# Expert results added in memory by the indirect stores, into three sums per token

## The chip, the cores and the metric

One core of a Trainium2 chip runs the whole program. The metric is the device time of one execution in microseconds (us); lower is better. The time of a kernel is the median of its runs.

## The reference, cut to what matters

One decoder layer over 16 sequences of 128 tokens with 256 features: a self-attention block, a cross-attention block and a feed-forward block, each followed by a layer norm. The change touches the last one, a mixture of 32 experts of which every token uses four, plus a shared expert:

```python
topk_idx, topk_w = _route(tokens, router_weight, router_bias)     # 4 of 32 experts per token
gate_vals = jax.nn.silu(jnp.einsum('th,eih->tei', tokens, gate_w))
up_vals = jnp.einsum('th,eih->tei', tokens, up_w)
expert_out = jnp.einsum('tei,ehi->teh', gate_vals * up_vals, down_w)
sel = jnp.take_along_axis(expert_out, topk_idx[:, :, None], axis=1)
mixed = (sel * topk_w[:, :, None]).sum(1)                          # the sum over the token's 4 experts
x = _layernorm(x + mixed + shared)
```

All 2048 tokens are routed; 2048 x 4 = 8192 expert results of 256 fp32 values (1 KB) have to be summed by token.

## The kernel before, in words

The kernel doesn't compute every expert for every token. During cross-attention each token's row is stored four times into the DRAM table `x_rows`, sorted by expert, by indirect stores that GpSimd issues (`scatter`, L1394). A row has 258 words: 256 words of token, then the row number where its result has to go, then its routing weight. Rows of an expert that no token fills are copies of a padding row, built in `padrow` (L343 to L345) and written to `pad_block` and to the end of `x_rows` by SyncE at the end of the first stage (L338, L339).

The expert stage (`expert_layer`) then runs over NT = 95 tiles of 128 rows: tile n < 32 is the first tile of expert n ("by expert"); the other 63 are taken from a table that the kernel works out ("by table"), with unused ones at the end that hold padding alone. For each tile, in a software pipeline over all engines:

- SyncE loads the tile's 129 KB of rows from `x_rows` into `xg` (L2081, 15 buffers).
- TensorE transposes the rows (L2304), multiplies by the expert's gate and up weights (L2255 by expert, L2286 by table), transposes the hidden values (L2296), multiplies by the down weights (L2315).
- ScalarE copies and applies silu (L2122, L2131, L2136). VectorE multiplies, splits into high and low halves (L2205, L2217), copies each tile's destination row numbers into `ix` (L2201) and moves the result from PSUM to `yo` (L2195, L2197; 8 buffers, each reused once the store that read it has landed, by the semaphore `stored`).
- GpSimd issues one indirect store per tile (L2097): row p of `yo` goes to row `ix[p]` of the DRAM table `y_rows`. Every (token, expert) pair has a row of its own, 4 per token. Padding rows have destination 1 << 20, which is over the bounds check, so that nothing is stored for them.

GpSimd does nothing else in this stage, and its instructions run in order.

When all 95 stores have landed, SyncE starts the tail (L2084 to L2089): 16 loads of 512 KB, one per 128 tokens, each with the four results of each token side by side, into four buffers `yg`. For each of these tiles GpSimd adds results 0 and 1 (`ya`, L2105), VectorE adds results 2 and 3 (`yb`, L2227), and TensorE sums three terms in PSUM by multiplying with the identity: `xs` (the residual with the shared expert in it, L2323), `ya` (L2325), `yb` (L2327). VectorE takes mean and variance (L2233 to L2239), GpSimd the inverse root (`frstd`, L2110), VectorE the shift (L2244), ScalarE scales (L2144) and stores 128 KB of output (L2146).

Of the kernel before, what the change touches and what calls it, by code (L numbers as in the profile page):

```python
# [6 lines left out]
F32 = mybir.dt.float32  # L7
F16 = mybir.dt.float16
BF16 = mybir.dt.bfloat16
ALU = mybir.AluOpType  # L10
# [3 lines left out]
U32 = mybir.dt.uint32  # L14

P = 128
D = 256
KT = D // P
NB = 16
# [9 lines left out]
TOPK = 4  # L29
# [9 lines left out]
NT = NE + NB * TOPK - 1  # L39
CAP = NB * P + P  # L40
BLOCKS = CAP // P
NDEST = NB * P * TOPK
RW = D + 2
PAD_DEST = 1 << 20
PAD = -3e38
TAKEN = 3e38
QK_SCALE = float(HD) ** -0.5
# [36 lines left out]
def wait(eng, sem, value):  # L84

    if not isinstance(value, int) or value > 0:
        eng.wait_ge(sem, value)


def live(n, count=NB):  # L90
    return 0 <= n < count
# [29 lines left out]
def decoder_kernel(nc, x, ctx_t, wcat, vecs, rowvecs, rel_bias, consts, masks, experts, rbias_d, out):  # L121
# [3 lines left out]
    with es:  # L125
# [5 lines left out]
        def sem(name):  # L131

            stage_sems.append(nc.alloc_semaphore(name=name))
            return stage_sems[-1]
# [32 lines left out]

        x_rows = nc.dram_tensor("x_rows", ((NE * BLOCKS + 1) * P, RW), U32, kind="Internal").ap()
        pad_block = nc.dram_tensor("pad_block", (P, RW), U32, kind="Internal").ap()
        y_rows = nc.dram_tensor("y_rows", (NDEST, D), F32, kind="Internal").ap()  # L170
        x_tiles = x.rearrange("b p d -> p b d")
        w_tiles = wcat.rearrange("(k p) c -> p k c", p=P)

        padded = sem("padded")
        idb_r = sem("idb_r")
        rc_in, k_in, id16_r, front_set = sem("rc_in"), sem("k_in"), sem("id16_r"), sem("front_set")
        ctx_in = [sem(f"ctx_in{k}") for k in range(2)]
# [19 lines left out]
        with ExitStack() as st:  # L197
# [107 lines left out]
            with nc.Block() as block:  # L305
                @block.sync
                def _(sp):
                    def piece(c):
                        t, col, width = W_PIECES[c]
                        wait_split(sp, c - WB)  # L310
                        sp.dma_start(wst[:, c % WB, :, 0:width], w_tiles[:, :, t * W1COLS + col:t * W1COLS + col + width]).then_inc(w_in[c % WB], 16)

                    sp.dma_start(xs[:, 0], x_tiles[:, 0]).then_inc(x_first, 16)
                    sp.dma_start(ident[:], consts[:, 0:P]).then_inc(const_in, 16)
                    sp.dma_start(vec[:], vecs).then_inc(const_in, 16)
                    sp.dma_start(par[:], masks).then_inc(const_in, 16)
                    sp.dma_start(rows[:, 4 * D:5 * D], rowvecs[4 * D:5 * D].rearrange("(a n) -> a n", a=1).broadcast_to([P, D])).then_inc(const_in, 16)
                    sp.dma_start(xs[:, 1:4, :], x_tiles[:, 1:4, :]).then_inc(x_in[0], 16)
                    for c in range(3, NPROJ):
                        piece(c)  # L320
                    sp.dma_start(xs[:, 4:8, :], x_tiles[:, 4:8, :]).then_inc(x_in[1], 16)
                    sp.dma_start(rows[:, 0:4 * D], rowvecs[0:4 * D].rearrange("(a n) -> a n", a=1).broadcast_to([P, 4 * D])
                                 ).then_inc(rows_in, 16)
                    sp.dma_start(rel[:].rearrange("p g h k -> p (g h k)"), rel_bias).then_inc(rel_in, 16)
                    for c in range(NPROJ, len(W_PIECES)):
                        piece(c)
                        if c in (8, 10):
                            k = {8: 2, 10: 3}[c]
                            sp.dma_start(xs[:, 4 * k:4 * k + 4, :], x_tiles[:, 4 * k:4 * k + 4, :]).then_inc(x_in[k], 16)
                    for n in range(FRONT):  # L330
                        sp.dma_start(cst[:, n], ctx_tiles[:, :, n]).then_inc(ctx_in[n], 16)
                    sp.dma_start(tri[:], consts[:, P:2 * P]).then_inc(rc_in, 16)
                    sp.dma_start(known[:], consts[:, 2 * P + NE:2 * P + 2 * NE + 1]).then_inc(k_in, 16)
                    sp.dma_start(first[:], consts[:, 2 * P:2 * P + NE]).then_inc(rc_in, 16)
                    sp.dma_start(dest_f[:].rearrange("p n k -> p (n k)"), consts[:, 2 * P + 2 * NE + 1:]).then_inc(rc_in, 16)
                    sp.dma_start(rbias[:], rbias_d.rearrange("(a n) -> a n", a=1).broadcast_to([P, NE])).then_inc(rc_in, 16)
                    sp.wait_ge(pad_set, 3)
                    sp.dma_start(pad_block, padrow[:]).then_inc(padded, 16)  # L338
                    sp.dma_start(x_rows[NE * CAP:NE * CAP + P, :], padrow[:]).then_inc(padded, 16)  # L339

                @block.gpsimd
                def _(pool):
                    pool.memset(padrow[:, 0:D], 0).then_inc(pad_set, 1)  # L343
                    pool.memset(padrow[:, D:D + 1], PAD_DEST).then_inc(pad_set, 1)
                    pool.memset(padrow[:].bitcast(F32)[:, D + 1:D + 2], 0.0).then_inc(pad_set, 1)  # L345
                    pool.memset(neghalf[:], -0.5).then_inc(setup, 1)
                    pool.memset(share[:], 2.0 / P).then_inc(setup, 1)
# [794 lines left out]
        c = Shared()  # L1142
# [10 lines left out]
        c.xv, c.xv_heads = xv, xv_heads  # L1153
        c.we_hi, c.we_lo = ([sb(f"{name}{j}", [P, 2, NE * EI], F16) for j in range(KT + 1)] for name in ("we_hi", "we_lo"))
        c.count = sb("count", [P, NE])
        c.pad_block, c.padded = pad_block, padded
        c.scattered = [sem(f"scattered{k}") for k in range(RR)]
        c.fill_row, c.fill_r, c.filled = sb("fill_row", [P, NE], U32), sem("fill_r"), [sem(f"filled{k}") for k in range(PAD_GROUPS)]
        cross_attention(nc, c, ctx_t, experts, consts, rbias_d, out)
# [806 lines left out]
def expert_layer(nc, c, st, consts, out):  # L1966
# [9 lines left out]
    L_GT, L_GU, L_SILU, L_TR = 2, 3, 4, 5  # L1976
    L_HI, L_DN, L_YO = (5, 6), (7, 8), (8, 9)
    LAG3 = L_YO[1]
    YS = 4

    def s3(name, shape, dt=F32):
        return st.enter_context(nc.sbuf_tensor(name, shape, dt))
# [29 lines left out]

    words = c.xT[:].rearrange("p n s k t -> p (n s k t)").bitcast(U32)
    xg = words[:, 0:G * RW].rearrange("p (g w) -> p g w", g=G)
    yg = words.bitcast(F32).rearrange("p (q d) -> p q d", q=YS)
    ya = s3("ya", [P, 2, D])
    yb = s3("yb", [P, 2, D])
    fin = s3("fin", [P, 4, D])
    fstats = s3("fstats", [P, 2, 6])
    fmv = s3("fmv", [P, 4, 2])  # L2020
# [7 lines left out]
    gu_ps, eg_r, eh_r, ehhi_r, ehlo_r = sem("gu_ps"), sem("eg_r"), sem("eh_r"), sem("ehhi_r"), sem("ehlo_r")  # L2028
    dn_ps, yo_r = sem("dn_ps"), sem("yo_r")
    stored = [sem(f"stored{k}") for k in range(YO)]  # L2030
    y_in = [sem(f"y_in{k}") for k in range(YS)]
    ya_r, yb_r, ysum_ps, fshift_r = sem("ya_r"), sem("yb_r"), sem("ysum_ps"), sem("fshift_r")
    f_stat, f_mv, f_var, f_rstd, fin_r = sem("f_stat"), sem("f_mv"), sem("f_var"), sem("f_rstd"), sem("fin_r")
    sent = [sem(f"sent{k}") for k in range(4)]

# [7 lines left out]
    def xg_word(dt, q, w):  # L2043
        return xg[:, q, D + w:D + w + 1].bitcast(dt)

    ix_r = sem("ix_r")
    tr_ps = sem("tr_ps")

    def by_expert(n):
        return live(n, NE)  # L2050
# [7 lines left out]
    def on_sync(sp, read_up_to, pad_rows):  # L2058
# [24 lines left out]
        for q in range(YO):  # L2083
            sp.wait_ge(stored[q], 16 * len(range(q, NT, YO)))  # L2084
        for n in range(NB):
            wait(sp, ya_r, n - YS + 1)
            wait(sp, yb_r, n - YS + 1)
            sp.dma_start(yg[:, n % YS], c.y_rows[n * P * TOPK:(n + 1) * P * TOPK, :].rearrange("(p k) d -> p (k d)", k=TOPK)
                         ).then_inc(y_in[n % YS], 16)  # L2089
        for p in range(4):  # L2090
            sp.wait_ge(sent[p], 16 * NB // 4)

    def on_gpsimd(pool):
        for n in range(NT):
            pool.wait_ge(ix_r, n + 1)
            pool.wait_ge(yo_r, n + 1)
            pool.indirect_dma_start(c.y_rows, bass.IndirectOffsetOnAxis(ap=ix[:, n % IX], axis=0),  # L2097
                                    yo[:, n % YO], None, bounds_check=NDEST - 1, oob_is_err=False).then_inc(stored[n % YO], 16)

        def final(i, p, h):  # L2100
            n = i
            if live(n):
                pool.wait_ge(y_in[n % YS], 16 * (n // YS + 1))
                wait(pool, ysum_ps, n - 1)
                pool.tensor_tensor(ya[:, n % 2], yg[:, n % YS, 0:D], yg[:, n % YS, D:2 * D], ALU.add).then_inc(ya_r, 1)  # L2105
            n = i - 2
            if live(n):
                pool.wait_ge(f_var, n + 1)
                wait(pool, fin_r, n - 3)
                pool.tensor_tensor(frstd[:, n % 4], fvar[:, n % 2], neghalf[:], ALU.pow).then_inc(f_rstd, 1)  # L2110

        unrolled(2, final)
# [72 lines left out]
    def on_vector(dve):  # L2185
        def tile(i, s, h):
# [11 lines left out]
            n = i - L_IX  # L2198
            if live(n, NT):
                dve.wait_ge(gathered[n % G], 16 * (n // G + 1))  # L2200
                dve.tensor_copy(ix[:, n % IX], xg_word(U32, n % G, 0)).then_inc(ix_r, 1)  # L2201
            for n in due(i, L_HI):
                dve.wait_ge(ehhi_r, n + 1)
                wait(dve, dn_ps, n - U + 1)
# [15 lines left out]
        unrolled(LAG3, tile, NT)  # L2220

        def final(i, p, h):
            n = i
            if live(n):
                dve.wait_ge(y_in[n % YS], 16 * (n // YS + 1))
                wait(dve, ysum_ps, n - 1)
                dve.tensor_tensor(yb[:, n % 2], yg[:, n % YS, 2 * D:3 * D], yg[:, n % YS, 3 * D:4 * D], ALU.add).then_inc(yb_r, 1)  # L2227
            n = i - 1
            if live(n):
                q = n % 2  # L2230
# [17 lines left out]
    def on_tensor(pe, shared_done):  # L2248
# [72 lines left out]
        for n in range(NB):  # L2321
            wait(pe, fin_r, n - 3)
            pe.matmul(SUM_BANK[n % 4][:, 0:D], ident[:], xs[:, n], start=True, stop=False)  # L2323
            pe.wait_ge(ya_r, n + 1)
            pe.matmul(SUM_BANK[n % 4][:, 0:D], ident[:], ya[:, n % 2], start=False, stop=False)  # L2325
            pe.wait_ge(yb_r, n + 1)
            pe.matmul(SUM_BANK[n % 4][:, 0:D], ident[:], yb[:, n % 2], start=False, stop=True).then_inc(ysum_ps, 1)  # L2327

    layer = Shared()
    layer.on_sync, layer.on_gpsimd, layer.on_scalar, layer.on_vector, layer.on_tensor = on_sync, on_gpsimd, on_scalar, on_vector, on_tensor  # L2330
# [18 lines left out]
def host_arrays(a):  # L2349
# [18 lines left out]
    place = np.arange(P, dtype=np.float32)  # L2368
    eye, earlier = np.eye(P, dtype=np.float32), (place[:, None] < place[None]).astype(np.float32)
    first_row = np.arange(NE, dtype=np.float32) * CAP  # L2370
    dest = ((np.arange(NB)[None, :, None] * P + np.arange(P)[:, None, None]) * TOPK + np.arange(TOPK)).reshape(P, NB * TOPK)
    consts = np.concatenate([eye, earlier, np.tile(first_row + 1, (P, 1)), place[:, None],
                             np.tile(np.arange(NE, dtype=np.float32), (P, 1)), dest], axis=1).astype(np.float32)

# [7 lines left out]
```

## Time and profile before

| | |
|---|---|
| time, median of 3 runs | 708.2 us (704.61 to 708.8) |
| the profiled execution: span from its first to its last instruction | 703.0 us; no other time of it is given |
| TensorE busy in the span | 579.9 us (82%) |
| VectorE, ScalarE, GpSimd busy | 515.3, 482.2, 475.9 us |
| indirect stores of results, L2097 | 95, 93.9 us busy, 988 ns each |
| first and last of them start at | 532.44 and 658.88 us |
| first tail load issued | 661.14 us |

The last instructions' stores to the output end after the last instruction that the span counts; what lies around the span is the difference between it and a run's time. The mean granted TensorE clock over the span is 0.948 of full speed.

### The profile page before, as it was taken

Reading aid. Unit: us, or ns where it says so; the run is one execution under the profiler, and the core shown is the slowest. Engines: PE = TensorE matmul, PEld = TensorE weight load, DVE = VectorE, ACT = ScalarE, POOL = GpSimd, SP = SyncE. Lnnn points to the kernel's source line nnn. Section 1 sums busy time; section 2 is a strip of 40 time slices with the busy share of each in tenths; the row PEclk is TensorE's granted clock in tenths of the full one; section 3 lists DMA queues with packets and bytes.
Section 4 is the critical chain, followed back from the end, with each engine's and each line's share of the span. In section 5 each row is a group of like instructions: output and inputs, shape, how many; then the busy total and the mean of one; then the engine's idle time right before and its main releaser. Section 6 shows DMA issues by size and latency. Waiting matters only on the chain.

```text
span 703.0 us, 24581 instructions
## 1 busy us (share of the span) xinstructions
PE 579.9 (82%) x8258; PEld 481.6 (69%) x8258; DVE 515.3 (73%) x2067; ACT 482.2 (69%) x1325; POOL 475.9 (68%) x622
## 2 busy tenths in 40 slices
PE   1799999999999864888888888766668999999393
PEld 1578888888888653656566656544558998889172
DVE  2898999889888632589999998654656776667274
ACT  3799999999899842577777777655236776666022
POOL 3667899999989973242668676453714777777584
PEclk9999999999999995899999999976899999999797
DMA  8420000000100001224464646322677556673394
GB/s 290 123 56 2 2 4 3 2 3 24 47 2 3 3 1 46 62 79 142 137 187 156 198 136 197 107 91 91 190 215 225 159 164 200 177 203 102 120 329 151
DMA packets 53643, 77.82 MB, mean 111 GB/s; under 512 B 8457, under 2 KB 42513, under 8 KB 52881
## 3 DMA queue, kind: packets, MB, share of 16 engines
q1 hardware_dynamic: 42768, 56.50, 27.5%
q0 software_dynamic: 7632, 16.87, 6.7%
q10 hardware_dynamic: 3120, 2.88, 1.2%
q8 instruction: 69, 1.13, 0.7%
q14 instruction: 54, 0.43, 0.2%
HBM read 48.62 MB, written 27.49 MB: 108 GB/s over the span
## 4 chain that ended last, share of the span: by engine, by line
PE 23%; DVE 18%; issue 9%; ACT 3%; POOL 3%; SPq 2%; DMA 2%; DVEq 0%; ACTq 0%; POOLq 0%
PE bank L2286 6%; DVE mnx L1545 4%; PE bank L2315 4%; PE bank L2304 2%; PE bank L2255 2%; DVE we_lo L1585 2%; PE bank L1770 2%; SPq L1314 2%; PE bank L1923 1%; DMA out<-fin 1%; PE bank L1842 1%; DVE min_hl L1552 1%; PE bank L2296 1%; PE bank L1819 1%; DVE min_hl L1554 1%
## 5 line engine op out<-in xcount | busy, mean ns | idle before, releaser
L2097 POOL DMA_INDIRECT y_rows<-front,ix x95 | 93.9, 988 | 52.5 <-DVE ix L2201 27.6
L566 ACT ACTIVATE sc<-sc,mn 128x128 f32<-128x128 f32 x256 | 82.6, 416 | 3.0 <-DVE mn L785 3.0
L1394 POOL DMA_INDIRECT x_rows<-rows,slot_ix x64 | 65.3, 1021 | 16.1 <-issue 12.8
L2122 ACT ACTIVATE gT<-bank 128x512 f16<-128x512 f16 x95 | 56.3, 595 | 27.3 <-DVE eh_lo L2205 21.7
L785 DVE CUSTOM_DVE_ANT_0 sc<-bank,rel 128x128 f32<-128x128 f32 x256 | 57.5, 285 | 0.8 <-issue 0.5
L794 DVE TENSOR_TENSOR pT_lo<-bank,pT_hi 128x512 f16<-128x512 f32 x64 | 43.1, 674 | 5.3 <-ACT pT_hi L573 5.2
L2197 DVE COPY front<-bank 128x256 f32<-128x256 f32 x63 | 26.7, 424 | 22.9 <-PE bank L2315 22.7
L1545 DVE TENSOR_REDUCE mnx<-bank 128x4 f32<-128x512 f32 x64 | 39.6, 680 | 4.1 <-PE bank L1819 4.0
L969 PE MATMUL bank<-hT,w_hi 128*128 128x128 f16 x384 | 41.4, 221 | 1.2 <-POOL hT L376 0.9
L573 ACT ACTIVATE pT_hi<-bank 128x512 f16<-128x512 f32 x64 | 38.5, 604 | 4.4 <-PE bank L928 4.1
L928 PE MATMUL bank<-ident,sc 128*128 128x128 f32 x256 | 39.4, 277 | 1.1 <-DVE k_lo L775 1.1
L2286 PE MATMUL bank<-we_hi,gT 128*128 x252 | 37.8, 273 | 1.5 <-ACT gT L2122 1.2
L2304 PE MATMUL bank<-ident,hT 128*128 128x128 f16 x380 | 36.5, 219 | 3.0 <-DMA hT<-x_rows 2.5
L1364 POOL TENSOR_TENSOR we_lo<-east,we_hi 128x256 f16<-128x256 f32 x48 | 31.3, 684 | 7.6 <-ACT we_hi L1427 7.4
L1459 ACT ACTIVATE pT<-bank 128x512 f32<-128x512 f32 x64 | 33.0, 601 | 4.5 <-PE bank L1845 4.1
L1372 POOL TENSOR_SCALAR xvar<-xmv 128x1 f32<-128x1 f32 x16 | 3.6, 227 | 46.6 <-DVE xmv L1609 46.6
L1770 PE MATMUL bank<-w_hi,front 128*128 128x256 f16 x120 | 25.1, 307 | 11.8 <-DVE front L1711 11.8
L952 PE MATMUL bank<-w_hi,hT 128*128 128x256 f16 (+1 forms) x128 | 31.8, 331 | 1.0 <-DVE vloc L744 0.8
L2144 ACT ACTIVATE fin<-bank,fshift,frstd 128x256 f32<-128x256 f32 x16 | 9.0, 565 | 34.3 <-DVE fshift L2244 25.2
L1427 ACT ACTIVATE we_hi<-east 128x256 f16<-128x256 f32 (+1 forms) x80 | 31.3, 456 | 0.0
L2304 PEld LDWEIGHTS bank<-ident,hT 128*128 128x128 f16 x380 | 27.7, 98 | 4.0 <-issue 3.3
L969 PEld LDWEIGHTS bank<-hT,w_hi 128*128 128x128 f16 x384 | 28.5, 99 | 2.3 <-DVE w_lo L700 1.3
(318 smaller groups left out, 2333.2 us busy)
## 6 DMA issues: line engine op xcount, KB each, us to landing
east<-in_experts SPq DMA_DIRECT2D x32, 384.0 KB, 3.3
hT<-x_rows SPq DMA_DIRECT2D x95, 129.0 KB
rows<-xhl SPq DMA_DIRECT2D x16, 512.0 KB, 4.1
hT<-y_rows SPq DMA_DIRECT2D x16, 512.0 KB, 5.5
x_rows<-pad_block SPq DMA_DIRECT2D x32, 129.0 KB, 2.6
wst<-in_wcat SPq DMA_DIRECT2D x8, 256.0 KB, 7.2
front<-in_ctx_t SPq DMA_DIRECT2D x16, 128.0 KB, 3.0
out<-fin ACTq DMA_DIRECT2D x16, 128.0 KB, 4.9
```

The source lines that it names most:

```text
L566: done = act.activation(sc[:, g, j], sc[:, g, j], ACT.Exp, bias=mn[:, n % 2, g, j:j + 1], scale=-1.0)
L785: dve.tensor_tensor_reduce(out=sc[:, g, j], in0=sc_bank[g][:, j * P:(j + 1) * P], in1=rel[:, g, j], scale=-1.0, scalar=-NEG, op0=ALU.add, ...
L794: dve.tensor_tensor(pT_lo[:, g % 2], pT_bank[g][:].rearrange("p (h k) -> p h k", h=GH), pT_hi[:, g % 2], ALU.subtract).then_inc(pT_rd[g], 1)
L928: last = pe.transpose(pT_bank[g][:, j * P:(j + 1) * P], sc[:, g, j], ident[:])
L969: last = pe.matmul(room[u][:, m * P:(m + 1) * P], w[:, k, col + m * P:col + (m + 1) * P], hT[:, n, hp, k], start=t == 0 and not bias, stop ...
L1394: pool.indirect_dma_start(shared.x_rows, bass.IndirectOffsetOnAxis(ap=slot_ix[:, n, k:k + 1], axis=0), rows4[:, q, k], None).then_inc(shar ...
L1545: dve.tensor_reduce(mnx[:, n % 2, g], sc_bank[g][:].rearrange("p (h k) -> p h k", h=GH), AX_X, ALU.min).then_inc(xmn_r[g], 1)
L1770: last = pe.matmul(room[u][:, m * width:(m + 1) * width], lhs(x_, k, m), rhs(y_, k, m), start=first and t == 0, stop=t == 5)
L2097: pool.indirect_dma_start(c.y_rows, bass.IndirectOffsetOnAxis(ap=ix[:, n % IX], axis=0), yo[:, n % YO], None, bounds_check=NDEST - 1, oob_ ...
L2122: act.activation(gT[:, n % U], GT_BANK[n % len(GT_BANK)], ACT.Copy).then_inc(gt_r, 1)
L2286: done = pe.matmul(GU_BANK[n % len(GU_BANK)][:, 0:2 * EI].rearrange("p (m w) -> p m w", m=2), gT[:, n % U, x_, k], E[y_][k][:, :, bass.ds( ...
L2304: done = pe.transpose(GT_BANK[n % len(GT_BANK)][:, part, k], xg.bitcast(F16)[:, n % G, (part * KT + k) * P:(part * KT + k + 1) * P], c.ide ...
```

## The change

The indirect stores add into memory (`compute_op=ALU.add`) instead of overwriting. `y_rows` holds three sums per token instead of four results: tile n adds into sum n mod 3, by adding n mod 3 to the destination row numbers when VectorE copies them. As every addition reads its row first, three things come with it. The table is cleared once, by a 6.7 MB store that SyncE issues at the end of the first stage from the zeros of `padrow`. Padding rows can't be skipped (the bounds check goes) and get 128 x 3 spare rows at the end of the table, one for each partition and sum. And GpSimd waits, ahead of store n, until store n - 3, the last one into the same sum, has landed. In the tail a load is 384 KB (three sums), there are five buffers instead of four, `yb` and its addition on VectorE are gone, and TensorE takes the third sum straight from the loaded tile.

```diff
-NDEST = NB * P * TOPK
+SUMS = 3
+NSUM = (NB * P + P) * SUMS
...
+                    sp.dma_start(y_rows.rearrange("(p k) d -> p k d", p=P), padrow[:, 0:D].bitcast(F32).unsqueeze(1).to_broadcast([P, NSUM // P, D])
+                                 ).then_inc(cleared, 16)
...
-                    pool.memset(padrow[:, D:D + 1], PAD_DEST).then_inc(pad_set, 1)
+                    pool.iota(padrow[:, D:D + 1], [[0, 1]], base=NB * P * SUMS, channel_multiplier=SUMS).then_inc(pad_set, 1)
...
-    YS = 4
+    YS = 5
...
+    def y_count(n):
+        return 16 * (len(range(n % YS, NT, G)) + n // YS + 1)
...
         for n in range(NB):
-            wait(sp, ya_r, n - YS + 1)
-            wait(sp, yb_r, n - YS + 1)
-            sp.dma_start(yg[:, n % YS], c.y_rows[n * P * TOPK:(n + 1) * P * TOPK, :].rearrange("(p k) d -> p (k d)", k=TOPK)
+            wait(sp, ysum_ps, n - YS + 1)
+            sp.dma_start(yg[:, n % YS], c.y_rows[n * P * SUMS:(n + 1) * P * SUMS, :].rearrange("(p k) d -> p (k d)", k=SUMS)
...
     def on_gpsimd(pool):
+        pool.wait_ge(c.cleared, 16)
         for n in range(NT):
             pool.wait_ge(ix_r, n + 1)
             pool.wait_ge(yo_r, n + 1)
+            if n >= SUMS:
+                pool.wait_ge(stored[(n - SUMS) % YO], 16 * ((n - SUMS) // YO + 1))
             pool.indirect_dma_start(c.y_rows, bass.IndirectOffsetOnAxis(ap=ix[:, n % IX], axis=0),
-                                    yo[:, n % YO], None, bounds_check=NDEST - 1, oob_is_err=False).then_inc(stored[n % YO], 16)
+                                    yo[:, n % YO], None, compute_op=ALU.add).then_inc(stored[n % YO], 16)
...
-                dve.tensor_copy(ix[:, n % IX], xg_word(U32, n % G, 0)).then_inc(ix_r, 1)
+                if n % SUMS:
+                    dve.tensor_scalar(ix[:, n % IX], xg_word(U32, n % G, 0), n % SUMS, None, ALU.add).then_inc(ix_r, 1)
+                else:
+                    dve.tensor_copy(ix[:, n % IX], xg_word(U32, n % G, 0)).then_inc(ix_r, 1)
...
-                dve.tensor_tensor(yb[:, n % 2], yg[:, n % YS, 2 * D:3 * D], yg[:, n % YS, 3 * D:4 * D], ALU.add).then_inc(yb_r, 1)
...
+            pe.wait_ge(y_in[n % YS], y_count(n))
+            pe.matmul(SUM_BANK[n % 4][:, 0:D], ident[:], yg[:, n % YS, 2 * D:3 * D], start=False, stop=False)
             pe.wait_ge(ya_r, n + 1)
-            pe.matmul(SUM_BANK[n % 4][:, 0:D], ident[:], ya[:, n % 2], start=False, stop=False)
-            pe.wait_ge(yb_r, n + 1)
-            pe.matmul(SUM_BANK[n % 4][:, 0:D], ident[:], yb[:, n % 2], start=False, stop=True).then_inc(ysum_ps, 1)
+            pe.matmul(SUM_BANK[n % 4][:, 0:D], ident[:], ya[:, n % 2], start=False, stop=True).then_inc(ysum_ps, 1)
...
-    dest = ((np.arange(NB)[None, :, None] * P + np.arange(P)[:, None, None]) * TOPK + np.arange(TOPK)).reshape(P, NB * TOPK)
+    dest = np.repeat((np.arange(NB)[None] * P + np.arange(P)[:, None]) * SUMS, TOPK, axis=1)
```

## Rows read from the trace of the kernel before

**Rows 1.** Timeline of GpSimd, indirect stores: start us, us, operation, idle before and releaser.
```profile
511.23 0.96 POOL L1394 DMA_INDIRECT x_rows<-rows,slot_ix  x1 [0.30 <-issue]
532.44 1.00 POOL L2097 DMA_INDIRECT y_rows<-front,ix  x1 [18.99 <-DVE ix L2201]
544.88 0.98 POOL L2097 DMA_INDIRECT y_rows<-front,ix  x1 [2.28 <-DVE ix L2201]
563.05 0.99 POOL L2097 DMA_INDIRECT y_rows<-front,ix  x1 [0.30 <-issue]
```

**Rows 2.** Timeline of TensorE and VectorE in the stage by table.
```profile
641.73 0.27 PE L2315 MATMUL bank<-we_lo,eh_hi 128*128 x1
642.04 0.42 DVE L2197 COPY front<-bank 128x256 f32<-128x256 f32 x1 [0.38 <-PE bank L2315]
642.38 0.14 DVE L2201 COPY ix<-hT 128x1 uint32<-128x1 uint32 x1
643.04 0.27 PE L2315 MATMUL bank<-we_lo,eh_hi 128*128 x1
```

**Rows 3.** Chain that ended last, from the last store on: start us, us, what.
```profile
658.88 2.11 DMA y_rows<-front,ix
661.14 3.52 DMA hT<-y_rows
665.75 1.22 PE bank L2325 x2
```

**Rows 4.** Stretches: length, busy us (PE, PEld, DVE, ACT, POOL), TensorE clock, DMA share, GB/s.
```profile
530.00:545.00 15.00, 12.46 (x196) 11.98 (x193) 9.01 (x39) 9.65 (x31) 8.15 (x9) 1.00 0.85 243
575.00:590.00 15.00, 14.60 (x156) 13.24 (x155) 10.47 (x46) 10.62 (x35) 11.50 (x12) 1.00 0.75 225
605.00:620.00 15.00, 14.65 (x156) 13.29 (x155) 10.36 (x44) 10.41 (x34) 11.35 (x13) 1.00 0.63 184
```

**Rows 5.** DMA issues in 530:545, 575:590, 605:620: operation, count, median us to landing.
```profile
y_rows<-front,ix POOLq DMA_INDIRECT x9, 4.0
...
y_rows<-front,ix POOLq DMA_INDIRECT x12, 2.7
...
y_rows<-front,ix POOLq DMA_INDIRECT x13, 3.2
```

**Rows 6.** DMA queue (packets, MB, share of 16 engines) and issues, 635:650, without loads.
```profile
q0 software_dynamic: 531, 1.32, 25.5%
...
y_rows<-front,ix POOLq DMA_INDIRECT x13, 2.5
```

**Rows 7.** DMA issues in 650:661: the last stores.
```profile
y_rows<-front,ix POOLq DMA_INDIRECT x8, 2.1
```

**Rows 8.** A stretch of the tail, columns as in group 4.
```profile
664.00:668.00 4.00, 2.25 (x5) 1.85 (x6) 0.99 (x3) 0.00 (x0) 1.96 (x3) 0.50 1.03 396
```

**Rows 9.** Groups by line in the tail: count, busy us, mean ns, idle before.
```profile
L2105 POOL TENSOR_TENSOR ya<-hT 128x256 f32<-128x256 f32 x16 | 13.1, 821 | 10.0 <-DMA hT<-y_rows 7.5 <-PE bank L2327 2.2
...
L2110 POOL TENSOR_TENSOR frstd<-fvar,neghalf 128x1 f32<-128x1 f32 x16 | 10.7, 668 | 1.1 <-DVE fvar L2239 0.9
```

**Rows 10.** Timeline of the tail: third tile's and last tile's last sum, GpSimd between.
```profile
671.53 0.59 PE L2327 MATMUL bank<-yb,ident 128*128 128x256 f32 x2
...
672.28 0.72 POOL L2105 TENSOR_TENSOR ya<-hT 128x256 f32<-128x256 f32 x1 [0.16 <-PE bank L2327]
...
692.21 0.59 PE L2327 MATMUL bank<-yb,ident 128*128 128x256 f32 x2
```

**Rows 11.** Timeline: SyncE's queue between its first two stages, DMA then, GpSimd's start.
```profile
179.29 0.83 SPq L339 DMA_DIRECT2D x_rows<-padrow  x1
269.78 0.90 SPq L1323 DMA_DIRECT2D front<-in_ctx_t  x2
...
193.00:211.00 18.00, 17.78 (x261) 15.26 (x258) 16.14 (x66) 17.42 (x53) 15.33 (x21) 1.00 0.01 2
...
9.70 0.57 POOL L369 TENSOR_SCALAR vareps<-mv 128x1 f32<-128x1 f32 x1 [7.53 <-DVE mv L723]
```

More of the change, by code:

```diff
@@ L41 @@
 BLOCKS = CAP // P
-NDEST = NB * P * TOPK
+SUMS = 3
+NSUM = (NB * P + P) * SUMS
 RW = D + 2
-PAD_DEST = 1 << 20
 PAD = -3e38
@@ L169, in decoder_kernel @@
         pad_block = nc.dram_tensor("pad_block", (P, RW), U32, kind="Internal").ap()
-        y_rows = nc.dram_tensor("y_rows", (NDEST, D), F32, kind="Internal").ap()
+        y_rows = nc.dram_tensor("y_rows", (NSUM, D), F32, kind="Internal").ap()
         x_tiles = x.rearrange("b p d -> p b d")
         w_tiles = wcat.rearrange("(k p) c -> p k c", p=P)
-        padded = sem("padded")
+        padded, cleared = sem("padded"), sem("cleared")
         idb_r = sem("idb_r")
@@ L1155, in decoder_kernel @@
         c.count = sb("count", [P, NE])
-        c.pad_block, c.padded = pad_block, padded
+        c.pad_block, c.padded, c.cleared = pad_block, padded, cleared
         c.scattered = [sem(f"scattered{k}") for k in range(RR)]
@@ L2014, in expert_layer @@
     xg = words[:, 0:G * RW].rearrange("p (g w) -> p g w", g=G)
-    yg = words.bitcast(F32).rearrange("p (q d) -> p q d", q=YS)
+    yg = words.bitcast(F32)[:, 0:YS * SUMS * D].rearrange("p (q d) -> p q d", q=YS)
     ya = s3("ya", [P, 2, D])
-    yb = s3("yb", [P, 2, D])
     fin = s3("fin", [P, 4, D])
@@ L2030, in expert_layer @@
     stored = [sem(f"stored{k}") for k in range(YO)]
-    y_in = [sem(f"y_in{k}") for k in range(YS)]
-    ya_r, yb_r, ysum_ps, fshift_r = sem("ya_r"), sem("yb_r"), sem("ysum_ps"), sem("fshift_r")
+    y_in = gathered[0:YS]
+    ya_r, ysum_ps, fshift_r = sem("ya_r"), sem("ysum_ps"), sem("fshift_r")
     f_stat, f_mv, f_var, f_rstd, fin_r = sem("f_stat"), sem("f_mv"), sem("f_var"), sem("f_rstd"), sem("fin_r")
@@ L2102, in final @@
             if live(n):
-                pool.wait_ge(y_in[n % YS], 16 * (n // YS + 1))
+                pool.wait_ge(y_in[n % YS], y_count(n))
                 wait(pool, ysum_ps, n - 1)
@@ L2222, in final @@
         def final(i, p, h):
[L2223 to L2226, printed above, removed]
-                dve.tensor_tensor(yb[:, n % 2], yg[:, n % YS, 2 * D:3 * D], yg[:, n % YS, 3 * D:4 * D], ALU.add).then_inc(yb_r, 1)
             n = i - 1
```

## The prediction, made before the changed kernel was run

> **What bounds the kernel now.** I read the busy shares first, then the timeline of each engine from 515 us on, the chain of waits, and the DMA shares by stretch; nothing ahead of the expert stage depends on the change but two small edits, costed below.
>
> In the expert stage the reader should see two engines at nearly the same pace. GpSimd issues the 95 stores of results, each 0.99 us long with 0.30 us to the next, a period of 1.29 us [rows 1]; TensorE's tiles by table come every 643.04 - 641.73 = 1.31 us [rows 2]. From the first store (532.44) to the last (658.88) [rows 1, 3] pass 126.4 us; 94 periods of 1.29 are 121.3. So GpSimd idles for only 5.2 us in the whole stage, 2.0 of it in one place (2.28 idle instead of 0.30, at 544.88 [rows 1]). The chain of waits ends the stage on it: the last store lands 2.11 us after its start, and the tail's first load is issued only then, at 661.14 [rows 3]. Every microsecond that the stores lose, beyond those 5.2, moves the end.
>
> In the tail 16 tiles pass. From the third tile's last product (671.53 + 0.59) to the last tile's (692.21 + 0.59) there are 13 tiles in 20.7 us, 1.59 us each [rows 10]. A tile moves 512 KB in and 128 KB out, 655,360 bytes, and where the DMA share is full it moves 396 GB/s [rows 8]: 1.65 us. The DMA engines set the pace there, which is what the change takes from.
>
> **The change, part by part.** The sum is made against the span of 703.0 us. The median of the runs shown, 708.2, is 5.2 above it, and I add these 5.2 at the end.
>
> *The tail.* A tile moves 384 + 128 KB, 524,288 bytes: 1.32 us at the same rate. Next slowest is GpSimd, one addition (821 ns mean) and one root (668) per tile, 1.49 [rows 9]; where it isn't pressed an addition takes 0.72 [rows 10], and with VectorE's own addition gone I take 0.73 + 0.67 = 1.40. TensorE's three products stay three. The pace falls from 1.59 to 1.40: 13 x 0.19 = 2.5 us (1.3 at 1.49, 3.5 at 1.32). Ahead of that, the first load lands at 661.14 + 3.52 = 664.66, and TensorE starts only at 665.75, after GpSimd's addition [rows 3]; it can now start with the loaded third sum: 1.1 us sooner, and 0.3 more as the load is a quarter shorter (128 KB at 396 GB/s). The granted clock is 0.50 here (1.2 GHz) [rows 8]; I assume that it rises as much sooner, else this gain shrinks towards nothing. Tail: **-3.9** (-1.3 to -5.5).
>
> *The store instruction.* No row shows an adding one. Its length: a store without a bounds check takes 0.96 [rows 1], so the period could be 1.27 at best; if adding doubled GpSimd's work on it, 0.99 more, 2.28. I take no change: 0.96 to 1.00 is what every store takes [rows 1], the ones of the last stretch too, which land like empty ones (2.1) [rows 7]. So its length doesn't follow what is written. The ends stay for the rivals.
>
> *The wait for store n - 3.* A met wait costs nothing: stores of the earlier stage that wait for nothing have the same 0.30 gap [rows 1]. It is unmet when a store lands later than three periods, 3.87 us less part of the 0.30 for issuing: I take 3.7. Queued behind it on GpSimd are only later stores; VectorE waits for them through the eight result buffers, then TensorE. Landings now: 2.1 for the last ones [rows 7], 2.5 without loads beside [rows 6], 2.7 and 3.2 at DMA shares of 0.75 and 0.63, 4.0 at 0.85 [rows 4, 5]. An adding store reads its 128 rows a second time. In the stretch without loads the stores take 25.5% of 15 us = 3.8 us for 1.32 MB, ten full stores of 131 KB: 0.38 each [rows 6]; that is my price of the second read (none, if it runs beside the first). Also 13 stores share these 3.8 us, 0.29 each, as padding is skipped; after the change all rows are moved, twice: 0.76. That adds 0.47 per 1.29 us, so a share of 0.63 becomes 0.99. So landing lies between 2.7 + 0.38 = 3.1 and 4.0 + 0.38 = 4.4; the nearest row by share is the crowded one, so I take the upper half, mean 4.1, a period of (4.1 + 0.17) / 3 = 1.42, with the same 0.17 for issuing.
> - The first 16 stores, in the crowded start: 4.4 gives 1.52, 16 x 0.23 = 3.7, of which the idle 2.0 absorb their part: +1.7 (0 to +4).
> - Some 62 stores with loads beside: 62 x 0.13 = **+8.1** (0 at 3.7 or less; +14 at 4.4).
> - The last 17, when loading has run ahead of the work: 2.5 + 0.38 = 2.9, no wait. Of the 3.2 us of idle time left, half absorbs: -1.6.
> - The last store is on the chain; its landing goes from 2.1 to 2.9: +0.8 (+0.4 to +2).
>
> *Covered edits, costed at nothing.* The clearing store, 6.7 MB, about 17 us at 396 GB/s, is issued after 179.29 + 0.83 us; SyncE's next DMA is at 269.78, and DMA is at 0.01 meanwhile [rows 11]. Five times slower would still be covered; without that cover GpSimd's first store would wait for it. The row numbers as iota: GpSimd is idle for 7.53 us before 9.70 [rows 11]. The addition to the row numbers instead of a 0.14 us copy, on 63 tiles: VectorE idles 0.38 per tile waiting for TensorE [rows 2]; without that, at most 63 x 0.14 = 9.
>
> Sum: 1.7 + 8.1 - 1.6 + 0.8 - 3.9 = +5.1; 703.0 + 5.1 + 5.2 = **713 us**. Its own range, from a landing of 3.7 to 4.4 and the tail's ends: 704 to 722.
>
> **The rivals.**
> - *The adding store keeps GpSimd longer* (slower). GpSimd writes what the DMA engines then execute, and an addition has two reads to write. Against it: the constant length above. It decides from 5.2 / 94 = 0.055 us per store on. For a third of a doubling, +0.33: 94 x 0.33 = 31, less 3.6 absorbed, + 0.8 - 3.9 = +24, no wait for landing as three periods are then 4.9: 732 us. The Trainium skill (GPSIMD Engine Reference, "4. When to use GPSIMD") says that one core of a pair emits the read descriptors and the other the write descriptors; by it the reading core's work would double. No run here shows which of the two sets the 0.99 us.
> - *The DMA engines saturate* (slower). At a share of 0.99 landing may pass every row; 5.0 us gives a period of 1.72, 78 x 0.43 = 33.5, less 3.6, + 0.8 - 3.9 = +27: 735 us. For it: 4.0 already now at 0.85. Against: loads run up to 15 tiles ahead and can give way.
> - *The second read is hidden and the window holds* (faster). Landing stays below 3.7, the stage is unchanged, only +0.5 at its end: 703.0 - 3.9 + 0.5 + 5.2 = 705 us; with the tail's best end 703, and with a period of 1.27 towards 701. For it: 2.1 empty against 2.5 full, so rows cost little. The Trainium skill (DMA: Bandwidth & Descriptors, "Anatomy of one DMA — SWDGE (gpsimd) path") puts a fixed 2.0 us, mostly the write receipt, beside bytes / 436e3; by it a full store lands at 2.3, with a second read 2.6, and no wait would ever be unmet. The trace agrees with no loads beside (2.5), not in the crowded stretch (4.0).
> - *The tail doesn't get shorter*, as GpSimd's 1.49 takes the pace: part of every case, the -1.3 above.
>
> **How the numbers follow.** About 1% (7 us: 701.1, 715.3) can be told from no change. Chances: my forecast 0.46 (0.30 within 1%, 0.16 above), longer instruction 0.22, saturation 0.10, hidden 0.22 (0.16 within 1%, 0.06 faster). So faster 0.06, same 0.46, slower 0.48; more of the slower half is one-sided, but no single slower case beats the forecast. Range: 701 to 738, which leaves out the best of the hidden case and the worse half of the slow rivals, 0.2.
>
> **What would show it.** Right: stores of about 0.99 us, idle time ahead of them put down to the landing of stores (about +0.1 us each), a stage about 9 us longer and 16 tail tiles about 4 us shorter, with no addition on VectorE. Wrong: a longer store instruction; gaps of 0.30 unchanged, with landings under 3.7; or TensorE waiting for loads of rows in the stage; or a tail that still paces at 1.59.

## The result: slower, 756.2 us, and the profile after

The changed kernel takes 756.17 us (752.73 to 759.4, 4 runs) against 708.5 for the kernel before on the same chip: a ratio of 1.0687, 95% interval 1.0639 to 1.0736. That is outside the predicted range of 701 to 738. Line numbers below are the changed kernel's: the store is L2103, a tail load L2091, the tail's products L2327 (`xs`), L2329 (third sum, as loaded) and L2331 (`ya`).

The profiled span went from 703.0 to 755.8 us, +52.8. First the page's group of the stores (count, busy us, mean ns, idle time before), then GpSimd's timeline, to set against [rows 1]:

```profile
L2103 POOL DMA_INDIRECT y_rows<-front,ix x95 | 147.6, 1553 | 53.0 <-DVE ix L2210 23.7
```

```profile
539.64 1.62 POOL L2103 DMA_INDIRECT y_rows<-front,ix  x1 [21.53 <-DVE ix L2210]
...
563.02 1.55 POOL L2103 DMA_INDIRECT y_rows<-front,ix  x1 [0.30 <-issue]
564.88 1.55 POOL L2103 DMA_INDIRECT y_rows<-front,ix  x1 [0.30 <-issue]
...
717.14 1.55 POOL L2103 DMA_INDIRECT y_rows<-front,ix  x1 [0.30 <-issue]
```

A store now keeps GpSimd for 1.55 us instead of 0.99. The gap behind it is still 0.30: nothing was put in front of the stores, they themselves are longer. The period is 1.86 us (564.88 - 563.02), and 94 of them are 174.8 us of the 177.5 from the first start to the last (126.4 before). The very first store, with none ahead of it, already took 1.62.

The waits of GpSimd and of VectorE from the first store on (us in total, times, longest):

```profile
POOL y_rows L2103 <- DVE ix L2210: 23.7, 7, 21.5
POOL y_rows L2103 <- issue: 22.8, 74, 0.6
POOL y_rows L2103 <- DVE ix L2208: 4.7, 10, 1.0
POOL y_rows L2103 <- DMA y_rows<-front,ix: 1.5, 3, 0.9
...
DVE front L2203 <- DMA y_rows<-front,ix: 51.4, 52, 2.3
DVE front L2201 <- DMA y_rows<-front,ix: 17.7, 17, 2.3
```

The wait that I forecast, GpSimd for the landing of store n - 3, is there 3 times, for 1.5 us in all. (Of the 23.7 us put down to the row numbers, 21.5 lie before the first store.) VectorE, which idled 0.38 a tile for TensorE [rows 2], now waits 69 us for stores to land, so that a result buffer comes free: it has run up against GpSimd.

The stage's end in the chain of waits, as in [rows 3] (start us, us, what):

```profile
717.14 3.71 DMA y_rows<-front,ix
...
721.01 3.35 DMA hT<-y_rows
...
724.40 1.22 PE bank L2329 x2
```

The last store lands 3.71 us after its start instead of 2.11. TensorE starts 3.39 us after the first load instead of 4.61, and on the loaded third sum (L2329), not on `ya`.

Stretches of the stage and one of the tail, columns as in [rows 4]:

```profile
540.00:555.00 15.00, 15.00 (x237) 14.59 (x235) 11.43 (x51) 11.84 (x37) 11.93 (x8) 1.00 0.98 215
575.00:590.00 15.00, 9.94 (x102) 7.56 (x100) 7.31 (x32) 6.47 (x21) 11.75 (x9) 1.00 0.83 139
605.00:620.00 15.00, 12.89 (x112) 10.44 (x112) 7.49 (x32) 7.36 (x25) 12.30 (x9) 0.89 0.88 134
635.00:650.00 15.00, 11.40 (x112) 9.23 (x112) 7.46 (x32) 7.10 (x24) 12.53 (x9) 1.00 0.92 144
732.00:745.00 13.00, 12.90 (x58) 10.51 (x58) 8.79 (x38) 5.08 (x10) 10.99 (x18) 1.00 0.97 347
```

The reader is to see two things. Past the crowded start TensorE gets through 102 to 112 products in 15 us, where it did 156 [rows 4]: it waits. And the DMA engines are busier (0.83 to 0.98, against 0.63 to 0.85) while they move fewer bytes per second than in [rows 4].

The tail, groups by line as in [rows 9] and TensorE's timeline as in [rows 10] (third tile's last product, last tile's):

```profile
L2111 POOL TENSOR_TENSOR ya<-hT 128x256 f32<-128x256 f32 x16 | 11.7, 730 | 9.8 <-DMA hT<-y_rows 7.8 <-PE bank L2331 1.7
L2116 POOL TENSOR_TENSOR frstd<-fvar,neghalf 128x1 f32<-128x1 f32 x16 | 8.8, 548 | 1.1 <-DVE fvar L2243 0.7
```

```profile
729.88 0.59 PE L2331 MATMUL bank<-ya,ident 128*128 128x256 f32 x2
...
732.47 0.59 PE L2331 MATMUL bank<-ya,ident 128*128 128x256 f32 x2
732.91 0.59 PE L2327 MATMUL bank<-xs,ident 128*128 128x256 f32 x2
733.34 0.59 PE L2329 MATMUL bank<-hT,ident 128*128 128x256 f32 x2
733.77 0.59 PE L2331 MATMUL bank<-ya,ident 128*128 128x256 f32 x2
...
747.46 0.59 PE L2331 MATMUL bank<-ya,ident 128*128 128x256 f32 x2
```

Thirteen tiles pass in 17.58 us, 1.35 each instead of 1.59; where nothing disturbs, a tile takes 1.30 (733.77 - 732.47), three products of 0.43 back to back: TensorE is the bound.

So the +52.8 are made of: first store at 539.64 instead of 532.44, +7.2; first to last store +51.1; last store to first load, 3.87 instead of 2.26, +1.6; first load to the last output store's issue, 721.01 to 750.81 instead of 661.14 to 695.59, -4.65; and from there to the end of the span, 5.0 instead of 7.4, -2.4.

The medians of the runs lie only 47.7 us apart, not 52.8. Every run of the changed kernel, and of the experiments, is 1.8 us longer than its span (757.6 and 755.8 for the profiled one). With 1.8 the profiled execution before would have taken 704.8, 3.7 under its kernel's median, and the changed kernel's took 1.4 over its own. So some 5 of the 52.8 are the choice of executions, and most of the 5.2 that the forecast added for what lies around the span are so too. Nor do output stores lie behind the span: the last one before lands 1.7 us after its issue at 695.59, well ahead of the span's end at 703.0.

### The profile page after: what moved, and what is told of

It is laid out like the page before. It is cut to its first block, busy times and chain, and to the rows that moved or that the text cites. A ratio compares the mean times of both kernels' runs of the same rounds, so it can differ in the third digit from the quotient of the medians.

```text
span 755.8 us, 24445 instructions
## 1 busy us (share of the span) xinstructions
PE 602.5 (80%) x8258; PEld 487.5 (65%) x8258; DVE 509.7 (67%) x2051; ACT 481.8 (64%) x1325; POOL 525.7 (70%) x622
## 3 DMA queue, kind: packets, MB, share of 16 engines
q0 software_dynamic: 16752, 20.92, 17.7%
## 4 chain that ended last, share of the span: by engine, by line
issue 18%; DVE 17%; PE 13%; DMA 7%; POOL 5%; ACT 2%; DVEq 0%; ACTq 0%; POOLq 0%; SPq 0%
DMA y_rows<-front,ix 6%; DVE mnx L1547 4%; POOL y_rows L2103 3%; PE bank L1772 2%; PE bank L1925 2%; DVE we_lo L1587 1%; PE bank L2259 1%; PE bank L1844 1%; DVE min_hl L1554 1%; PE bank L1821 1%; PE bank L2331 1%; PE bank L2329 1%; DVE min_hl L1556 1%; DVE xstats L1608 1%; PE bank L2319 1%
## 5 line engine op out<-in xcount | busy, mean ns | idle before, releaser
L2103 POOL DMA_INDIRECT y_rows<-front,ix x95 | 147.6, 1553 | 53.0 <-DVE ix L2210 23.7
L1461 ACT ACTIVATE pT<-bank 128x512 f32<-128x512 f32 x64 | 33.2, 601 | 6.4 <-PE bank L1847 5.9
L2300 PE MATMUL bank<-ident,eh 128*128 128x128 f32 x63 | 18.6, 296 | 22.6 <-DVE eh L2226 22.1
L1772 PE MATMUL bank<-w_hi,front 128*128 128x256 f16 x120 | 27.4, 332 | 11.2 <-DVE front L1713 11.2
L2319 PE MATMUL bank<-we_hi,eh_hi 128*128 (+1 forms) x95 | 26.3, 277 | 6.7 <-DVE front L2201 3.7
```

Source lines behind the costliest of these rows:

```text
L1772: last = pe.matmul(room[u][:, m * width:(m + 1) * width], lhs(x_, k, m), rhs(y_, k, m), start=first and t == 0, stop=t == 5)
```

## The experiments

My theory after the result was G: GpSimd's adding instruction is itself longer, and that is nearly all. Its rivals were W (the window's wait), D (the DMA engines, which hold GpSimd back) and C (the clearing store).

### One part at a time

**Plain stores in the changed kernel** (a1_plain):

```diff
-                                    yo[:, n % YO], None, compute_op=ALU.add).then_inc(stored[n % YO], 16)
+                                    yo[:, n % YO], None).then_inc(stored[n % YO], 16)
```

> The changed kernel with plain indirect stores in place of adding ones; clearing, spare rows for padding, the wait for store n - 3 and the shorter tail stay (a sum then holds one of its results only). Theory G (GpSimd itself takes longer over an adding store: 1.55 us against 0.99): the store falls to 0.96 to 0.99 us, its period to 1.27 to 1.31, the stage from first to last store from 177.5 to about 126 us, the time to 756 - 51 = 702 to 707 us. Theory P (it is the padding rows, which are no longer skipped, or the missing bounds check): stores stay at 1.55 us, the time at 756. Theory W (the wait for store n - 3): the wait is still there, and all 128 rows are moved; landings over 3.7 us would leave a period over 1.35 and a time over 710.

Measured: 719.61 us, ratio to the kernel before 1.0134 (1.0059 to 1.0209); 37 us of the 48 are gone, but not all, as G's 702 to 707 had it. The group of the stores and GpSimd's wait:

```profile
L2103 POOL DMA_INDIRECT y_rows<-front,ix x95 | 91.2, 960 | 70.4 <-DVE ix L2210 25.3
...
POOL y_rows L2103 <- DMA y_rows<-front,ix: 18.5, 25, 2.1
```

The store is back at 0.96, with the padding rows moved and no bounds check, so theory P falls. But with it the window's wait appears, 25 times, 18.5 us, and from the first store to the last pass 139.1 us. The chain shows one such wait, a store that starts 0.11 us after another has landed:

```profile
601.35 4.12 DMA y_rows<-front,ix
605.47 0.02 issue
605.50 0.04 POOLq L2102
605.54 0.04 issue
605.58 0.61 POOL y_rows L2103
```

**Adding stores alone** (a2_add_only): the kernel before, with four results per token, rows of its own for every (token, expert) pair, no window and the old tail; the stores add, the padding goes to spare rows and the table is cleared.

```diff
-                                    yo[:, n % YO], None, bounds_check=NDEST - 1, oob_is_err=False).then_inc(stored[n % YO], 16)
+                                    yo[:, n % YO], None, compute_op=ALU.add).then_inc(stored[n % YO], 16)
```

> The kernel before with adding stores and nothing else of the change: four results per token, each row added to once, padding into eight sets of spare rows taken in turn, so that no store has to wait for store n - 3; the table is cleared first; the tail is that of before. Theory G: stores of 1.55 us, period 1.86, stage 177 us, and the tail's 7 us are not gained: 756 + 7 = 763 us. Theory W: without the wait the period goes back to about 1.3 and the time to 708 to 715 us.

Measured: 756.82 us, ratio 1.0655 (1.0595 to 1.0716), the whole loss without any window. It is 6 us under G's 763: the old tail is here only 4.4 us longer than the changed kernel's (34.2 against 29.8), not 7, and the first store starts 3 us sooner.

```profile
L2102 POOL DMA_INDIRECT y_rows<-front,ix x95 | 147.7, 1555 | 48.3 <-DVE ix L2208 26.0
```

From the first store to the last pass 176.7 us, against 177.5 with the window. So the window costs nothing that can be told while the instruction is this long: three periods are 5.6 us, and GpSimd met a landing later than that only 3 times, for 1.5 us.

**The clearing store alone** (a3_clear_only): the kernel before, which clears a table that nobody reads.

```diff
+                    sp.dma_start(y_clear.rearrange("(p k) d -> p k d", p=P), padrow[:, 0:D].bitcast(F32).unsqueeze(1).to_broadcast([P, (NB + 1) * 3, D])
```

> The kernel before with a 6.7 MB clearing store to a table that nothing reads, issued where the change issues its own, and GpSimd's wait for it. If the clear is covered: 708.5 us within 0.5%, first result store at 532 us within 2. Theory C (the changed kernel's first store came 7 us later, at 539.6, because of the clear): 713 to 716 us and a first store near 539.

Measured: 707.81 us, ratio 0.999 (0.995 to 1.003). C falls. Here too the first store started late, at 538.8 us; over all the kernels of this study it starts between 532.4 and 539.6, plain or adding, cleared or not. So the 7.2 us of later start are not the change's.

### What the instruction's length follows

Three kernels cut what a store moves (results are left out of the sums in the first two, half of each result in the third).

**64 rows, adding and plain** (b1_add_64_rows, b2_plain_64_rows), the adding one's edit:

```diff
-            pool.indirect_dma_start(c.y_rows, bass.IndirectOffsetOnAxis(ap=ix[:, n % IX], axis=0),
-                                    yo[:, n % YO], None, compute_op=ALU.add).then_inc(stored[n % YO], 16)
+            pool.indirect_dma_start(c.y_rows, bass.IndirectOffsetOnAxis(ap=ix[0:P // 2, n % IX], axis=0),
+                                    yo[0:P // 2, n % YO], None, compute_op=ALU.add).then_inc(stored[n % YO], 16)
```

> The changed kernel with adding stores of 64 rows: each leaves out the tile's upper 64 rows. Theory G, with a cost per row: the 0.57 us that adding costs halves to 0.28 over a plain store of 64 rows; if all of the 1.55 us goes by rows, 0.78. With a cost per instruction: 1.55 stays.

> The same with plain stores of 64 rows. With b1 and the two kernels of 128 rows it gives fixed part and part per row of a plain and of an adding store. All by rows: 0.49 us. All fixed: 0.97 to 0.99.

**Rows half as wide** (b3_add_half_width): all 128 rows, 512 B of each, added into a table of its own.

```diff
+            pool.indirect_dma_start(c.y_half, bass.IndirectOffsetOnAxis(ap=ix[:, n % IX], axis=0),
+                                    yo[:, n % YO, 0:D // 2], None, compute_op=ALU.add).then_inc(stored[n % YO], 16)
```

> The changed kernel with adding stores of 128 rows of 128 values (512 bytes instead of 1 KB): the second half of each result is left out, in a table of its own, and the tail reads the other, cleared one. Theory G (the price is for rows, which GpSimd writes one by one): 1.55 us and a period of 1.86 stay, the time stays at 752 to 759. Theory D (GpSimd is held up by the DMA engines, which add at a third of the speed at which they copy: 65% of 20 us for 10.7 full stores, 1.21 us each, against 0.38): half the bytes take half as long, the store falls towards 1.2 us and the time to about 725.

One run each: 743.11, 703.08 and 751.25 us. The stores' group and the queue of GpSimd's DMAs (packets, MB, share of 16 engines) of each, in that order, and of the changed kernel and the one with plain stores:

```profile
q0 software_dynamic: 10672, 14.69, 11.2%
L2103 POOL DMA_INDIRECT y_rows<-front,ix x95 | 133.6, 1407 | 50.1 <-DVE ix L2210 19.2
```

```profile
q0 software_dynamic: 6112, 14.69, 6.4%
L2103 POOL DMA_INDIRECT y_rows<-front,ix x95 | 85.4, 899 | 63.2 <-DVE ix L2210 22.9
```

```profile
q0 software_dynamic: 16752, 14.69, 11.9%
L2106 POOL DMA_INDIRECT y_half<-front,ix x95 | 147.6, 1553 | 50.9 <-DVE ix L2213 22.5
```

```profile
q0 software_dynamic: 16752, 20.92, 17.7%
```

```profile
q0 software_dynamic: 7632, 20.92, 7.9%
```

Half the bytes leave the instruction at 1553 ns, while the queue's DMA share falls from 17.7 to 11.9%: D falls, the length doesn't hang on what the DMA engines carry. Half the rows take it to 1407 adding and 899 plain, 0.51 apart, neither the 0.28 of an extra that goes by rows alone nor the 1.55 of one that is all fixed. By rows alone, (1552 - 1402) / 64 = 2.3 ns a row adding, by the stores' typical lengths, and (960 - 897) / 64 = 1.0 plain; without rows that leaves 1.25 and 0.83 us.

**32 rows, adding** (c3_add_32_rows), to test that line: the same edit with P // 4.

> The changed kernel, with each adding store cut to the first 32 rows of its tile (the other 96 results are left out of the sums). Measured so far: adding stores 1.552 us at 128 rows and 1.402 at 64; plain ones 0.960 and 0.897. Theory G (a fixed part of the addition on GpSimd and a part by row): on the line through 1.552 and 1.402 the store takes 1.25 + 32 x 0.00234 = 1.33 us, 0.43 more than a plain one's line gives without rows, a period of 1.63, so with 94 periods 153 us from first to last start and about 731 us in all. Rival (the length follows the rows alone, and 64 rows is a step): 1.2 or less, 720 or less, where TensorE's period of 1.31 comes in sight.

Measured: 734.69 us (one run).

```profile
q0 software_dynamic: 7632, 11.58, 7.9%
L2103 POOL DMA_INDIRECT y_rows<-front,ix x95 | 124.3, 1308 | 52.7 <-DVE ix L2210 21.6
```

79 of the 95 took 1.30 us; the line said 1.33. The time is 4 us above the 731 that the line gave. The stage has 1 of them (154.1 us from first to last store against 153, with 39 waits for landings, 13.1 us, that the shorter store makes up for), and the end of the span 2.5 (last section). This kernel's queue has the same 7632 packets as that of the plain stores of 128 rows, at 0.96 us. So it is not the count of packets alone either: an addition costs some 0.4 us whatever it adds, and about 1.4 ns more for each row, together the 0.59. Whether that smaller part goes by rows or by packets stays open, as an adding store puts every row into a packet of its own (last section).

### The window and the padding rows

**Plain stores that move the padding too, without a window** (c1_plain_all_rows), to split the 13 us by which plain stores behind the window are slower than the kernel before:

```diff
-PAD_DEST = 1 << 20
+PAD_DEST = NDEST
...
-                                    yo[:, n % YO], None, bounds_check=NDEST - 1, oob_is_err=False).then_inc(stored[n % YO], 16)
+                                    yo[:, n % YO], None).then_inc(stored[n % YO], 16)
```

> The kernel before with one thing of the change: its plain stores lose the bounds check, so that padding rows are moved too (to spare rows, eight sets, one for each store in flight); the clearing store stays. Four results per token, no wait for store n - 3, the old tail. It tells where the 13 us come from by which the plain stores behind the window (139.1 us from first to last start) stay behind the kernel before (126.4). Theory W (the window's wait makes them): store 0.96, gap 0.30, from first to last start 119 to 127 us, tail 41 to 42, so 701 to 709. Rival P (moving the padding rows loads the DMA engines, so that loads of rows come late, with or without a window): some 139 us as behind the window, with idle time of GpSimd put down to the row numbers or to VectorE, and 717 to 724.

Measured: 707.0 us, ratio 0.998 (0.9937 to 1.0023).

```profile
532.51 0.96 POOL L2102 DMA_INDIRECT y_rows<-front,ix  x1 [18.92 <-DVE ix L2208]
...
657.57 0.96 POOL L2102 DMA_INDIRECT y_rows<-front,ix  x1 [0.30 <-issue]
```

125.1 us from first to last, against 126.4 before: moving the padding rows costs nothing that can be told beside the 94 x 0.03 = 2.8 us that the store gains at most by losing the bounds check. The stage itself varies by some 2 us: with the stores of before and the clearing store alone it took 124.2. So rival P falls, and the 14.0 us between 125.1 and 139.1 go with the window. Three rows per token instead of four, VectorE's edit of the row numbers and the tail differ too, but only behind the window does GpSimd wait for landings (18.5 us).

**A window of two** (c2_window_two), with adding stores:

```diff
-            if n >= SUMS:
-                pool.wait_ge(stored[(n - SUMS) % YO], 16 * ((n - SUMS) // YO + 1))
+            if n >= 2:
+                pool.wait_ge(stored[(n - 2) % YO], 16 * ((n - 2) // YO + 1))
```

> The changed kernel with the window one store tighter: store n waits until store n - 2 has landed, not n - 3. All else as changed. Two periods of 1.857 are 3.71 us, and the adding stores' landings measured where any was shown are 3.2 to 3.7, 5.8 in the crowded start. Theory G (GpSimd's adding instruction of 1.55 us sets the stage, and landings of adding stores are mostly under 3.6): 756 to 764, idle time put down to landings under 10 us. Rival S (the DMA engines are a second wall: with their share at 0.9 and over, landings are 4 to 4.5): a period of 2.1 to 2.3, 94 x 0.25 to 0.45 = 23 to 42 us more: 780 to 798.

Measured: 804.93 us, ratio 1.1374 (1.1314 to 1.1433), slower than either theory had it. From the first store (537.38) to the last (765.05) pass 227.7 us, 2.42 each. Landings, from the DMA issues of 655 to 675 us (count, median us to landing), and that stretch, columns as above:

```profile
y_rows<-front,ix POOLq DMA_INDIRECT x8, 3.8
```

```profile
655.00:675.00 20.00, 13.24 (x112) 9.95 (x111) 7.53 (x32) 7.48 (x24) 12.15 (x8) 0.91 0.65 106
```

The chain of waits shows every second store, each two behind the one before it:

```profile
554.08 3.86 DMA y_rows<-front,ix
...
558.76 4.11 DMA y_rows<-front,ix
...
563.62 3.78 DMA y_rows<-front,ix
```

An adding store lands after 3.8 us with the DMA share at 0.65, where plain ones took 3.2 at 0.63 and 2.5 without loads [rows 4 to 6]. Of the 83 landings that the whole trace has, 65 took 3.6 to 4.0 us and 18 more. So rival S's landings of 4 to 4.5 by saturation are the exception, and G's of under 3.6 aren't there. The stores take 1.55 us here too, though GpSimd idles ahead of most of them and never has more than two on the way, which speaks against D once more.

Two periods are 4.84 us, 1.0 more than the median landing. After a landing the store that waited for it starts 0.75 us later (558.76 + 4.11, then 563.62), where the plain store shown under a1_plain started after 0.11; others of that run took 0.77 (588.34 + 3.15, then 592.26). The profile puts VectorE's two instructions into that time, though the row numbers are made tiles ahead; what fills it stays open.

No kernel here beats the one before by an amount that can be told from the spread of the runs. The third sum saves its 3 to 5 us of tail, but every way tried of getting the sums costs more.

## Why the prediction was wrong, step by step

- **The store instruction: the step that failed.** "I take no change: 0.96 to 1.00 is what every store takes" and "So its length doesn't follow what is written". It took 1.55: 94 x (1.552 - 0.986) = +53.2 us, of which 2.1 went into idle time, leaves the +51.1. The rows behind the argument couldn't bear it. The stores of the last stretch that land "like empty ones" write next to nothing, yet they put as many packets into the queue as any other: the kernel before sends 7632 in all, the same as when padding is moved as well (a1_plain, c1_plain_all_rows). What I held constant was constant in every row I looked at: all were plain stores of 128 rows. And what the length does follow, whether the store adds and how many rows it has, varied in none. The bounds, 0.96 to 1.98, held the value; choosing the end that the most rows repeat, for an operation of which no row existed, was the mistake.
- **The rival that came true** was "the adding store keeps GpSimd longer". Its place and its course are right (GpSimd's instruction, almost no wait for landing, three periods pass the landing), its size too small: I took a third of a doubling, +0.33, and 732 us; with +0.57 the same working gives 53.2 - 3.6 + 0.8 - 3.9 = +46.5, that is 754.7. The Trainium skill (GPSIMD Engine Reference, "4. When to use GPSIMD") has one core emit read descriptors and the other write descriptors; no run here looks inside the two. The rival's reason, two reads to write, isn't shown: most of the extra, 0.4 of 0.59 us, isn't by row, as a doubled list of reads would be. What the fixed part is stays open.
- **The window's wait**: forecast as +8.2 us; it costs nothing that can be told behind adding stores (a2_add_only against the changed kernel). Behind plain stores of 0.96 the stage is 14.0 longer (139.1 against 125.1), near the upper end I gave, and that with no second read at all. So the mechanism was right for the instruction I assumed, and the longer instruction covers it. The landings in the forecast had a thin base, though: the trace before has them for every eighth store only, one or two in a stretch.
- **The second read** was priced at 0.38 us of all 16 DMA engines. The queue's time over the span is 17.7% of 755.8 = 133.8 us with adding stores and 7.9% of 716.7 = 56.6 with plain ones of the same bytes: 77.2 / 95 = 0.81 more per store, twice the price. The share reached 0.83 to 0.98, near the forecast 0.99, but what was late in the end wasn't loads: TensorE shows no wait for them from 540 to 717 us.
- **The tail**: -3.9 forecast, -4.65 measured to the last output store (and -3.2 to -5.5 when the other kernels' tails, 33.2 to 34.5 us old and 29.0 to 30.0 new, are set against each other). The pace is 1.35 a tile against 1.40 forecast, which gives 3.1 us for 2.5; the third tile's last product starts 8.87 us after the first load instead of 10.39, 1.5 sooner for 1.4. The granted clock rose sooner, as I assumed, with TensorE busy without a break from its first product on: it is 0.50 (1.2 GHz) from 726 to 729 us and 0.97 in the 3 us behind, so it rose about 8 us after the first load; before it is 0.50 from 668 to 670 and 0.71 in the 2 us behind, about 10 us after. TensorE became the bound, not GpSimd, whose root fell to 548 ns from 668 [rows 9]. It takes 548 to 553 in the seven kernels with the new tail and 649 to 689 in the four with the old; which part of the tail's change does it isn't separated.
- **The last landing** went from 2.11 to 3.71, +1.6, at the upper part of +0.4 to +2.
- **The covered edits** cost nothing that shows: the clearing store alone makes 0.999 of the time (0.995 to 1.003). VectorE's addition to the row numbers is lost in its 69 us of new waiting.

## What to carry to other kernels

An indirect store that adds is not a plain one with a different opcode: measure its length on the issuing engine before building on it, and where that engine already sets the pace, expect the stage to stretch by the difference times the count. When a trace holds no row of an operation, rows that agree with each other say nothing of it; ask what they all have in common (here plain stores of 128 rows) and whether the new operation keeps it. A wait that an experiment finds to be free may only be covered by the other cost of the same change: take that away and measure again, as with the window here.

## What the runs showed of the hardware

- **An adding indirect store on GpSimd** takes 1.30, 1.40 and 1.55 us for 32, 64 and 128 rows, a plain one 0.90 and 0.96 for 64 and 128. The width of an adding store's rows doesn't matter (512 B or 1 KB: 1.55).
- **Packets.** Dropping 64 rows from each of 95 plain stores takes 7632 - 6112 = 1520 packets away, 16 a store: four rows of 1 KB share a packet. From adding stores it takes 16752 - 10672 = 6080, 64 a store: every row is a packet, at 512 B too. Up to 530 us, ahead of these stores, the queue has 3072 packets, so a store of 128 rows has 48 plain and 144 adding, 16 of them beside those of the rows in either case; what these 16 are isn't shown. The Trainium skill (DMA: Bandwidth & Descriptors, "SWDGE vs HWDGE vs iDMA") says that a packet holds at most 4096 B preferably; the plain stores agree, the adding ones stay at one row.
- **DMA engine time**: the whole stores take 1.17 us of all 16 engines adding ((133.8 - 22.8) / 95) and 0.36 plain ((56.6 - 22.8) / 95), three times as much for the same bytes; 22.8 is the earlier stage's part, 4.3% of the first 530 us. The Trainium skill (Collectives: The Full Stack, "The bandwidth ceiling: the fold count and why AG ≠ RS ≠ AR") gives ReduceScatter, which adds, half the rate of AllGather, which copies, because an addition reads two sources; these indirect stores differ by a factor of three. A tile's loads take 0.56 us (8 loads, 29.9% of the engines from 575 to 590 us of the changed kernel), so behind GpSimd's 1.86 us a tile stands a second wall of some 1.73, an estimate from these rows. No run takes GpSimd's part away to show it.
- **The end of the span**, from the last output store's issue, is 5.0 us in the four kernels whose queue has 16752 packets and 7.4 to 7.5 in all the others, whatever the tail. Why is open; it gave the changed kernel 2.4 us back.
